# Two of four members of the middle feed-forward steps through split float32r down products, with one ring of six for the scan operands

## The reference, cut to what matters

```python
x = x + 0.5 * ffn(layernorm(x), w_gate, w_up, w_down)
x = x + attn(layernorm(x), ...)
x = x + 0.5 * ffn(layernorm(x), w_gate, w_up, w_down)

def ffn(x, w_gate, w_up, w_down):           # H = 512, I = 2048
    h = silu(x @ w_gate) * (x @ w_up)
    g = h.reshape(B, S, I // 4, 4)          # the two of largest magnitude of each four stay
    return keep_two_of_four(g).reshape(B, S, I) @ w_down

def step(h, inps):                          # the scan of the state-space part, E = 1024, N = 16
    d_l, b_l, c_l, u_l = inps
    h = exp(d_l[..., None] * A) * h + (d_l * u_l)[..., None] * b_l[:, None, :]
    return h, einsum('ben,bn->be', h, c_l)
```

## Time and profile before

| | us |
|---|---|
| median of 3 runs (3605.13 to 3610.43) | 3607.98 |
| profiled execution, time | 3602.44 |
| its span | 3600.7 |
| what lies around the span | 1.7 |
| busy: PE, DVE, POOL, ACT | 3360.2, 3027.7, 2594.9, 2061.7 |

### The profile page before, as it was taken

How to read it: one execution, slowest core, us unless ns; L and a number is a source line. 1 busy time by engine, 2 the same in 40 slices (tenths; PEclk the granted TensorE clock), 3 DMA queues, 4 the chain that set the end, 5 groups by cost and what they waited for, 6 DMA issues and landing times. The chain is left out here.

```text
span 3600.7 us, 39012 instructions
## 1 busy us (share of the span) xinstructions
PE 3360.2 (93%) x11958; PEld 2122.7 (59%) x12020; DVE 3027.7 (84%) x3597; ACT 2061.7 (57%) x2805; POOL 2594.9 (72%) x1625
## 2 busy tenths in 40 slices
PE   8999999999999999999999999988989889988899
PEld 6775566556655665566555565555545555555467
DVE  5546998788999889988898899988998988999934
ACT  5546657567565765566565675565555566454422
POOL 1316876667877779768787678868888878979913
PEclk9999999999999999999999999999999989999999
DMA  9656566657756676566665675647646556645433
GB/s 356 219 188 192 176 207 222 205 176 221 215 175 210 202 227 200 171 203 208 187 205 176 202 230 169 221 138 215 222 124 210 172 178 220 187 149 184 139 120 114
DMA packets 243470, 696.45 MB, mean 193 GB/s; under 512 B 23536, under 2 KB 23792, under 8 KB 233584
## 3 DMA queue, kind: packets, MB, share of 16 engines
q1 hardware_dynamic: 173632, 559.72, 45.1%
q10 hardware_dynamic: 69632, 134.23, 15.6%
HBM read 619.94 MB, written 76.55 MB: 193 GB/s over the span
## 5 line engine op out<-in xcount | busy, mean ns | idle before, releaser
L1381 POOL TENSOR_TENSOR scan_in<-du,scan_rows 128x512 f32<-128x512 f32 x1024 | 1312.8, 1294 | 700.9 <-DVE decay L1255 612.1
L1255 DVE TENSOR_TENSOR_SCAN decay<-decay,scan_in 128x512 f32<-128x512 f32 x1024 | 1252.4, 1223 | 157.0 <-ACT decay L865 150.9
L865 ACT ACTIVATE decay<-delta,small 128x512 f32<-128x512 f32 x1024 | 699.4, 689 | 935.4 <-DVE scan_out L1265 928.7
L1394 POOL TENSOR_TENSOR y<-y,scan_out 128x1024 f32<-128x1024 f32 x512 | 1227.0, 2397 | 0.6 <-DVE scan_out L1265 0.6
L637 PE MATMUL main<-zhi,wunit 128*128 128x512 f32 x2048 | 909.9, 444 | 62.1 <-DVE cmp L1195 38.3
L729 PE MATMUL side<-h,wdown 128*128 128x512 f32 x1760 | 801.8, 599 | 24.2 <-ACT sq L988 12.6
L639 PE MATMUL main<-zhi,wunit 128*128 128x512 f32 x2048 | 817.7, 399 | 0.0
L638 PE MATMUL main<-zlo,wunit 128*128 128x512 f32 x2048 | 816.7, 399 | 0.0
L1265 DVE TENSOR_TENSOR scan_out<-decay,scan_rows 128x512 f32<-128x512 f32 x1024 | 702.9, 686 | 27.6 <-POOL y L1394 2.2
L729 PEld LDWEIGHTS side<-h,wdown 128*128 128x128 f32 x1760 | 334.5, 191 | 392.7 <-issue 350.2
L637 PEld LDWEIGHTS main<-zhi,wunit 128*128 128x128 f32 x2048 | 390.2, 191 | 233.6 <-issue 89.5
(11 more groups left out here) (117 smaller groups left out, 3192.8 us busy)
## 6 DMA issues: line engine op xcount, KB each, us to landing
wunit<-hl_dram SPq DMA_DIRECT2D x480, 512.0 KB, 4.3
scan_rows<-bc_dram ACTq DMA_DIRECT2D x256, 512.0 KB, 5.7
wdown<-down_w_dram SPq DMA_DIRECT2D x256, 256.0 KB, 3.2
wmam<-mam_dram SPq DMA_DIRECT2D x128, 512.0 KB, 4.1
hl_dram<-wunit SPq DMA_DIRECT2D x32, 512.0 KB, 4.6
skip_dram<-skb SPq DMA_DIRECT2D x64, 256.0 KB, 4.2
delta<-skip_dram SPq DMA_DIRECT2D x16, 1024.0 KB, 6.7
wmam<-wout_dram SPq DMA_DIRECT2D x32, 512.0 KB, 4.3
```

Source lines behind the costliest of these rows:

```text
L865: nc.scalar.activation(decay[u % BANKS][:], delta[:, e, :], ACT.Exp, scale=aneg[:, e * N + n:e * N + n + 1]).then_inc(sem["decay_ready"], 1)
L1255: nc.vector.tensor_tensor_scan(decay[u % BANKS][:], decay[u % BANKS][:], db[u % INPUTS][:], 0.0, ALU.mult, ALU.add).then_inc(sem["state_re ...
L1381: nc.gpsimd.tensor_tensor(db[u % INPUTS][:], du[:, e, :], rows[m % ROWS][:, 0, :], ALU.mult).then_inc(sem["input_ready"], 1)
L1394: nc.gpsimd.tensor_tensor(y[:, e:e + 2, :], y[:, e:e + 2, :], scan_out[:, k:k + 2, :], ALU.add).then_inc(sem["sum_ready"], 1)
```

## The change

The 55 middle steps split members 0 and 1 (`SPLIT = 2`), and those halves of the down weights, into upper and lower parts. ACT copies the upper part of a member into `hmid` in the tick of its select, and that of `wdown[t]` (members 0 and 1, 128x256) into `wmid[t]` three ticks ahead of the down product; POOL subtracts one tick later, in place over `h` and `wdown` (`hlow`, `wlow`), at the head of the tick, before the tick's scan inputs. A down product becomes two float32 matmuls (members 2, 3) and six float32r ones. To make room, `scan_in` (four) and `scan_out` (six) become one ring of six: an input is written to a place, the scan reads it, `times_c` overwrites it, `sum_states` reads it. The input of unit u now also waits for the sum of unit u - 6, and LAG goes from 3 pairs to 2. The plan of ticks and units stays as it is. The diff, cut to its core (blank lines and most context left out):

```diff
@@ -31,9 +31,9 @@
 UNITS = 2 * HALF
-INPUTS, RING = 4, 6
-
-LAG = 3
+RING, AHEAD_OF_STATES = 6, 4
+
+LAG = 2
 BANKS = 2
@@ -72,6 +72,9 @@
 AHEAD_OF_SCANS = 5
+
+MIDDLE = tuple(s for s in range(4 * 2 * B) if s not in EDGE)
+SPLIT = 2
@@ -317,10 +320,10 @@
         rows = [scan_rows[:, 2 * k:2 * k + 2, :] for k in range(ROWS)]
-        scan_in = sb("scan_in", [P, INPUTS, L])
-        scan_out = sb("scan_out", [P, RING, L])
-        db = [scan_in[:, k, :] for k in range(INPUTS)]
-        pr = [scan_out[:, k, :] for k in range(RING)]
+        scan_ring = sb("scan_ring", [P, RING, L])
+        ring = [scan_ring[:, k, :] for k in range(RING)]
+        hmid = sb("hmid", [P, SPLIT, L], r32)
+        wmid = [sb(f"wmid{k}", [P, SPLIT, P], r32) for k in range(KD)]
         cv = [sb(f"cv{k}", [P, L]) for k in range(2)]
@@ -330,9 +333,12 @@
         aneg = small[:, C_AL:C_AL + KE * N]
-        hhi = nc.alloc_sbuf_tensor_at("hhi", [P, 4, L], r32, offset=base_of["scan_in"])
-        hlo = nc.alloc_sbuf_tensor_at("hlo", [P, 4, L], r32, offset=base_of["scan_out"])
-        count = nc.alloc_sbuf_tensor_at("count", [P, 3, L], bf16, offset=base_of["scan_out"] + 4 * L * 4)
+        hhi = nc.alloc_sbuf_tensor_at("hhi", [P, 4, L], r32, offset=base_of["scan_ring"])
+        hlo = nc.alloc_sbuf_tensor_at("hlo", [P, 4, L], r32, offset=base_of["scan_ring"] + 4 * L * 4)
+        count = nc.alloc_sbuf_tensor_at("count", [P, 3, L], bf16, offset=base_of["scan_ring"] + 8 * L * 4)
+
+        hlow = [nc.alloc_sbuf_tensor_at(f"hlow{k}", [P, 4, L], r32, offset=base_of[f"h{k}"]) for k in range(2)]
+        wlow = [nc.alloc_sbuf_tensor_at(f"wlow{t}", [P, 4, P], r32, offset=base_of[f"wdown{t}"]) for t in range(KD)]
         wparts = [nc.alloc_sbuf_tensor_at(f"wparts{k}", [P, 2, 4, P], r32, offset=base_of["scan_rows"] + k * 2 * L * 4) for k in range(ROWS)]
@@ -343,7 +349,7 @@
             "product_ready", "side_ready", "gate_read", "up_read", "part_ready",
-            "magnitude_ready", "compared", "counted", "selected",
+            "magnitude_ready", "compared", "counted", "selected", "mid_high_ready", "mid_split_ready", "wmid_high_ready", "wmid_split_ready",
             "member_high_ready", "member_split_ready", "down_high_ready", "down_split_ready",
@@ -396,6 +402,14 @@
                     if plan.base[s] + (3 + j // 2 if s in COUNTED else WIN_TICKS[j] + 1) == tick]
+
+        def middle_weights(tick):
+
+            return [(i, t) for i, s in enumerate(MIDDLE) for t in range(KD) if plan.base[s] + DOWN_TICKS[t] - 3 == tick]
+
+        def middle_members(tick):
+
+            return [(i, j) for i, s in enumerate(MIDDLE) for j in range(SPLIT) if plan.base[s] + WIN_TICKS[j] + 1 == tick]
@@ -725,8 +739,15 @@
                 pe.wait_ge(sem[f"down_loaded_{t}"], 16 * (s + 1))
-                for j in range(4):
-                    mm = nc.tensor.matmul(bank[:], wdown[t][:, j, :], h[s % 2][:, j, :], start=(j == 0), stop=(j == 3))
+                for j in range(SPLIT, 4):
+                    nc.tensor.matmul(bank[:], wdown[t][:, j, :], h[s % 2][:, j, :], start=(j == SPLIT), stop=False)
+                i = MIDDLE.index(s)
+                pe.wait_ge(sem["mid_split_ready"], SPLIT * (i + 1))
+                pe.wait_ge(sem["wmid_split_ready"], KD * i + t + 1)
+                for j in range(SPLIT):
+                    nc.tensor.matmul(bank[:], wmid[t][:, j, :], hmid[:, j, :], start=False, stop=False)
+                    nc.tensor.matmul(bank[:], wlow[t][:, j, :], hmid[:, j, :], start=False, stop=False)
+                    mm = nc.tensor.matmul(bank[:], wmid[t][:, j, :], hlow[s % 2][:, j, :], start=False, stop=(j == SPLIT - 1))
                 mm.then_inc(sem["side_ready"], 1)
@@ -944,10 +965,25 @@
                 if i == AHEAD_OF_SCANS:
+                    wait_job(act, ("down", MIDDLE[-1], KD - 1))
                     act.wait_ge(sem["state_ready"], B * UNITS)
                     act.wait_ge(sem["sum_ready"], B * UNITS // 2)
                 wait_selected(act, s, j)
                 nc.scalar.activation(hhi[:, j, :], h[s % 2][:, j, :], ACT.Copy).then_inc(sem["member_high_ready"], 1)
+
+            def middle_high(i, j):
+
+                s = MIDDLE[i]
+                wait_job(act, ("down", s - 1, KD - 1))
+                wait_selected(act, s, j)
+                nc.scalar.activation(hmid[:, j, :], h[s % 2][:, j, :], ACT.Copy).then_inc(sem["mid_high_ready"], 1)
+
+            def middle_down_high(i, t):
+
+                s = MIDDLE[i]
+                act.wait_ge(sem[f"down_loaded_{t}"], 16 * (s + 1))
+                wait_job(act, ("down", s - 1, t if i else KD - 1))
+                nc.scalar.activation(wmid[t][:], wdown[t][:, 0:SPLIT, :], ACT.Copy).then_inc(sem["wmid_high_ready"], 1)
@@ -1090,6 +1126,10 @@
                     down_high(i, t)
+                for i, j in middle_members(tick):
+                    middle_high(i, j)
+                for i, t in middle_weights(tick):
+                    middle_down_high(i, t)
                 upto(share(units, 1, 4).stop)
@@ -1209,6 +1249,8 @@
                     dve.wait_ge(sem["selected"], 4 * i)
+                else:
+                    wait_job(dve, ("down", MIDDLE[-1], KD - 1))
                 nc.vector.tensor_tensor(count[:, 0:2, :], cmp[:, 1:3, :], cmp[:, 3:5, :], ALU.add).then_inc(sem["counted"], 1)
@@ -1252,7 +1294,7 @@
                 dve.wait_ge(sem["input_ready"], u + 1)
-                nc.vector.tensor_tensor_scan(decay[u % BANKS][:], decay[u % BANKS][:], db[u % INPUTS][:], 0.0, ALU.mult,
+                nc.vector.tensor_tensor_scan(decay[u % BANKS][:], decay[u % BANKS][:], ring[u % RING][:], 0.0, ALU.mult,
                                              ALU.add).then_inc(sem["state_ready"], 1)
@@ -1260,9 +1302,7 @@
                 dve.wait_ge(sem["state_ready"], u + 1)
-                if u >= RING:
-                    dve.wait_ge(sem["sum_ready"], (u - RING) // 2 + 1)
-                nc.vector.tensor_tensor(pr[u % RING][:], decay[u % BANKS][:], rows[m % ROWS][:, 1, :], ALU.mult).then_inc(sem["weighted_ready"], 1)
+                nc.vector.tensor_tensor(ring[u % RING][:], decay[u % BANKS][:], rows[m % ROWS][:, 1, :], ALU.mult).then_inc(sem["weighted_ready"], 1)
@@ -1376,9 +1416,11 @@
                     pool.wait_ge(sem[f"rows_loaded_{m % ROWS}"], 16 * (m // ROWS + 1))
-                if u >= INPUTS:
-                    pool.wait_ge(sem["state_ready"], u - INPUTS + 1)
-                nc.gpsimd.tensor_tensor(db[u % INPUTS][:], du[:, e, :], rows[m % ROWS][:, 0, :], ALU.mult).then_inc(sem["input_ready"], 1)
+                if u >= RING:
+                    pool.wait_ge(sem["sum_ready"], (u - RING) // 2 + 1)
+                if u >= AHEAD_OF_STATES:
+                    pool.wait_ge(sem["state_ready"], u - AHEAD_OF_STATES + 1)
+                nc.gpsimd.tensor_tensor(ring[u % RING][:], du[:, e, :], rows[m % ROWS][:, 0, :], ALU.mult).then_inc(sem["input_ready"], 1)
@@ -1391,12 +1433,23 @@
                     pool.wait_ge(sem["sum_ready"], p - HE // 2 + 1)
-                nc.gpsimd.tensor_tensor(y[:, e:e + 2, :], y[:, e:e + 2, :], scan_out[:, k:k + 2, :], ALU.add).then_inc(sem["sum_ready"], 1)
+                nc.gpsimd.tensor_tensor(y[:, e:e + 2, :], y[:, e:e + 2, :], scan_ring[:, k:k + 2, :], ALU.add).then_inc(sem["sum_ready"], 1)
             def member_low(i, j):
                 pool.wait_ge(sem["member_high_ready"], 4 * i + j + 1)
                 nc.gpsimd.tensor_tensor(hlo[:, j, :], h[EDGE[i] % 2][:, j, :], hhi[:, j, :], ALU.subtract).then_inc(sem["member_split_ready"], 1)
+
+            def middle_low(i, j):
+
+                s = MIDDLE[i]
+                pool.wait_ge(sem["mid_high_ready"], SPLIT * i + j + 1)
+                nc.gpsimd.tensor_tensor(hlow[s % 2][:, j, :], h[s % 2][:, j, :], hmid[:, j, :], ALU.subtract).then_inc(sem["mid_split_ready"], 1)
+
+            def middle_down_low(i, t):
+
+                pool.wait_ge(sem["wmid_high_ready"], KD * i + t + 1)
+                nc.gpsimd.tensor_tensor(wlow[t][:, 0:SPLIT, :], wdown[t][:, 0:SPLIT, :], wmid[t][:], ALU.subtract).then_inc(sem["wmid_split_ready"], 1)
@@ -1430,6 +1483,10 @@
                     down_low(i, t)
+                for i, j in middle_members(tick - 1):
+                    middle_low(i, j)
+                for i, t in middle_weights(tick - 1):
+                    middle_down_low(i, t)
                 for u in plan.units_at[tick]:
                     scan_input(u)
                     if u % 2 == 1:
```

## The result

The changed kernel takes 3901.6 us (median of 4 runs, 3897.6 to 3903.7) against 3606.6 for the kernel before: ratio 1.0822, 95% interval 1.0809 to 1.0836, 295 us slower. The prediction of 3636 (3562 to 3706) had the sign and missed the size: 34 us over the profiled execution were forecast, 295 measured. The profiled execution's span is 3895.8 us.

A forecast was written before the change was run, and what follows sets the result against it. PE was taken to set the pace for the first two thirds, DVE after. From 3602.4 us, -50 (PE) +37 (overfull windows) +20 (stalls) +10 (ACT) +4 (port) +13 (lost lead) gave +34: 3636 us, range 3562 to 3706.

The forecast's parts named there:

- PE's saving: Down products of middle steps: 0.32 us less each, 69 us over 55 steps, booked at -50 for 40 steps with room.
- The ring: Scan buffers: sums waiting for times_c and LAG 2 taken to cost 0, bounds 0 and 20 us.
- POOL's work: New subtractions in middle steps: 5.5 us a step, 303 us over 55 steps (280 to 425).
- The wait behind the selects: POOL at base+5 waits for DVE's selects: 3.5 us stall, 73 us in 30 steps, booked at 20.
- overfull windows: 15 of 53 middle-step windows where POOL's old plus new work exceeds the window, by 37 us together.
- the waits for the weight copies: Lead lost at base+4, base+6 and base+7, where weight halves head POOL's tick: 0.25 us a step, +13.
- ACT: New copies, 2.9 us a step, 160 us in all, lengthen DVE's waits for decays: +10, bounds 0 and 45.
- The shared port: Busier POOL delays DVE operations on two SBUF tiles: +4 us, bounds 0 and 15.
- The clock: Last third: PE's pauses might pull down its granted clock, making the full loss worse; no size given.
- the rival of a full loss: Stalls paid in full at base+5, PE's saving given back: +73 and +37, 3712 us, chance 0.17.
- The one of a gain: Stalls vanish into DVE's waits for PE, PE's saving stays: about 3570 us, chance 0.28.
- The one of a dearer float32r: float32r inside a float32 accumulation has its own price on PE: +84 us, 3686, part of the 0.17.

The follow-up runs named there:

- run 4: Changed kernel with neither weights nor members split after the first middle step; PE's new matmuls and the ring stay; 3602.1 us, ratio 0.9989.
- the ring alone: Kernel before with only the ring of six and LAG 2; middle-step down products stay float32; 3610.1 us, ratio 1.0012.
- run 8: As run 4, no splits, but all four members in float32r, read from the first step's upper parts; 3596.1 us, ratio 0.9976.
- run 13: Changed kernel with members split only in the first middle step, weight copies two ticks earlier, weight subtractions behind the tick's scan inputs; 3647.8 us.
- run 2: Changed kernel with down weights split only once, before the first middle step; members split as in the changed kernel; 3787.1 us.
- run 3: Changed kernel with members split only once, in the first middle step; weights split as in the changed kernel; 3812.0 us.
- run 7: Changed kernel with weight copies two ticks earlier, weight subtractions behind the tick's scan inputs, and member subtractions moved to DVE; 3747.6 us.
- run 5: Changed kernel with ACT's copies of the weight halves two ticks earlier, all work and POOL's subtraction ticks kept; 3869.7 us.

## Why the prediction was wrong, step by step

The terms of the sum against the runs: PE's saving, booked at -50 us, is worth -8 (run 4 against the ring alone). The ring, booked at 0, costs 5. All that the splits bring to ACT and POOL was booked at 84 us (37, 20, 10, 4 and 13) and costs 299 (the changed kernel against run 4). So most of the miss, 215 us, lies in the price of the splits, and 42 in PE's saving.

**PE's saving** was right as work and wrong as time. A down product takes 3.12 us (443.19 to 446.31, which is the last start and one pitch of 0.23) against 3.44, the 0.32 forecast:

```profile
443.19 1.88 PE L743 MATMUL side<-h,wdown 128*128 128x512 f32 x4
444.51 0.80 PE L748 MATMUL side<-hmid,wmid 128*128 128x512 f32 x1
...
446.08 0.39 PE L750 MATMUL side<-hlow,wmid 128*128 128x512 f32 x1
```

The sum booked -50 us for 40 steps; against the ring alone run 4 gives -8, and run 8 some -13 for twice as much. The step that failed first is this one: from "PE is busy for 96%" I concluded that PE sets the pace. PE, DVE and ACT are levelled, and each waits now and then for another: relief of PE alone is worth 3 to 8 us, of DVE alone 41 of 89, of ACT's table loads 37, and PE's is worth 20 only on top of ACT's. In a plain step (step 7) DVE is busy for 39.1 of 40.8 us, and 1.2 of the rest is waiting for decays; PE's 39.0 stood beside it, not ahead of it.

**POOL's work** was right: 0.79 us for a weight half (0.74 forecast), 1.32 for a member, 317 us in all (303).

```profile
L1452 POOL TENSOR_TENSOR wlow<-wdown,wmid 128x256 fp32r<-128x256 f32 x220 | 174.1, 793 | 344.4 <-ACT wmid L986 325.1 <-DVE decay L1297 19.2
L1447 POOL TENSOR_TENSOR hlow<-h,hmid 128x512 fp32r<-128x512 f32 x110 | 142.9, 1320 | 122.3 <-ACT hmid L979 122.3
```

With next to no wait, the weight halves' 174 us of it cost 46 us together with ACT's copies (run 13).

**The wait behind the selects** was named, placed and sized rightly for a plain step (3.5 us forecast, 3.59 seen), and then booked at a quarter of its worth. This is the step that cost most. I counted 73 us, halved what fell outside the overfull windows, and took 20. The changed kernel shows 229.7 us at scans, and 28.1 more where DVE's gating of y (line 1335) waits for POOL's last sum, 1.9 before. Put to their ticks by the plan, 81.3 of the 229.7 us stand at `base+5`, so the 73 were about right and the discount was wrong. Another 17.7 stand at `base+4` and 91.2 at `base+6` and `base+7`, where the prediction had 13. With members alone (run 2) it is 58.9 at `base+5`; with weights alone (run 3) 11.3 there and 74.1 at the two ticks behind. Three things were missing. First, the waits for the weight copies, at the heads of three more ticks of each step: the prediction said of them only 0.25 us a step. Runs 3 and 13 price them, with what they do to DVE's busy time, at 164 us when they stand alone. Second, a lead of four units is lost at each gate and has to be won back, out of the little that POOL is faster than DVE in the dense ticks as far as the rows tell; step 8 shows further stalls of 0.71, 0.68, 1.64 and 0.70 us behind the first. Third, POOL's standing still and its work are in series. The 15 "overfull windows" took the larger of two times where the sum of POOL's work and its idle time at the gate was due, as step 7 shows (43.0 and 7.2 us in 50.2).

**ACT** was put at 10 us. Its copies took 0.40 and 0.63 us as forecast, but DVE's waits for decays went down, from 151 to 135. Its part is that of the one that POOL waits for (447 us). What its copies cost as work was not tried alone.

**The ring** was right at 0: 5 us, within 0 to 20.

**The shared port** was mis-sized. I took 4 us with an upper bound of 15; DVE's busy time grew by 108 us. Two groups hold most of it (busy us, mean ns of one), the first two rows from the kernel before, the other two from the changed one:

```profile
L1295 DVE TENSOR_TENSOR y<-y,delta 128x512 f32<-128x512 f32 x64 | 51.9, 871 | 13.2 <-DMA delta<-skip_dram 11.3 <-POOL y L1394 1.9
L1159 DVE TENSOR_TENSOR zlo<-zm,zhi 128x512 fp32r<-128x512 f32 x64 | 49.5, 834 | 0.0
L1335 DVE TENSOR_TENSOR y<-y,delta 128x512 f32<-128x512 f32 x64 | 96.2, 1561 | 29.2 <-POOL y L1436 28.1 <-DMA delta<-skip_dram 1.1
L1199 DVE TENSOR_TENSOR zlo<-zm,zhi 128x512 fp32r<-128x512 f32 x64 | 81.3, 1329 | 0.4 <-ACT zhi L945 0.4
```

They are DVE instructions with two SBUF operands, and nothing in them was changed. The error was to scale with POOL's busy share. What counts is whether POOL is at work just then. Of these 128 instructions, those with no POOL instruction beside them take 0.68 us in both kernels, those with one 1.96 before and 1.86 after; there were 17 of the second kind before and there are 83 now. A POOL that is behind works straight on through the ticks where it used to stand waiting for DVE. This agrees with the rule of the Trainium skill that the prediction weighed ("SBUF — State Buffer", Who interferes with whom); how often the two meet in a kernel, only the rows tell. The scans, whose decay lies in PSUM, are untouched as forecast: 1.223 us in the mean before, 1.225 after. What part of the 295 us the port makes was not tried apart from the rest, and this rival of the waits stays open in size. In run 7 the same effect on 110 new instructions is 0.67 us each (1.355 less the 0.68 of such an operation undisturbed), 74 us.

**The clock** is the last term. PE's busy time grew although its work fell: the mean granted clock of the execution is 0.946 against 0.979. From 452.44 on, after 5.97 us of waiting for DVE, the matmuls follow each other at 0.43 us, from 459.81 on again at 0.23:

```profile
452.44 0.79 PE L651 MATMUL main<-zhi,wunit 128*128 128x512 f32 x1 [5.97 <-DVE cmp L1235]
453.03 0.63 PE L652 MATMUL main<-zlo,wunit 128*128 128x512 f32 x1
453.45 0.63 PE L653 MATMUL main<-zhi,wunit 128*128 128x512 f32 x1
...
460.05 0.40 PE L653 MATMUL main<-zhi,wunit 128*128 128x512 f32 x1
460.28 0.39 PE L651 MATMUL main<-zhi,wunit 128*128 128x512 f32 x1
```

Two windows around these rows, columns as above, have the granted clock at 0.50 and 1.00, which are the two levels of 1.2 and 2.4 GHz:

```profile
452.40:456.00 3.60, 3.56 (x8) 2.81 (x9) 3.60 (x5) 1.36 (x3) 3.47 (x3) 0.50 0.02 5
459.40:462.00 2.60, 2.53 (x11) 2.07 (x12) 2.50 (x4) 2.48 (x4) 1.72 (x2) 1.00 0.90 297
```

Here the low clock follows a stall. What it adds to the 295 us no run parts; the rival of a full loss named it without a number.

**The rivals.** The one of a gain fell: DVE did wait, and PE had nothing to gain by. The one of stalls paid in full decided as it said, no gain on PE and stalls that stay. Its price of 110 us (3712) was 190 short of the 3901.6; the waits for the weight copies, the port and the clock are what it left out, and their shares are not parted. The one of a dearer float32r fell with run 8 and the 3.12 us. What could have been read beforehand: each subtraction at the head of a POOL tick has a partner on ACT in the tick before, and POOL's tick is tied to ACT's at all four of them. A lead of four units is 1.7 ticks where 2.3 units stand in a tick (1024 units on 448 ticks). I followed it through only one of the four gates.

## What to carry to other kernels

An engine that runs ahead of the others in its own queue does so only until its first instruction that needs something of the present: before work is given to its idle time, list every new wait with the tick of its producer, and count the lead as lost at each. With the copy early and the subtraction behind the work that others wait for, the same instructions cost 46 us instead of 210 (runs 13 and 3). And a busy share of 96% doesn't show which engine sets the pace; leaving out the helpers' work (run 4) shows in one run that the saving, with the ring, is worth 3 us.

## What the runs showed of the hardware

A wait taken away from a queue can reappear at the next gate in nearly its full length: 325 us at the weight copies became 241 us more at the members (run 5), with 32 us of gain. DVE's subtraction of two SBUF tiles of 128x512 took 0.68 us with no POOL instruction beside it and 1.55 in the mean with one (run 7), while scans with one operand in PSUM kept their 1.22 us. Going from float32 to float32r inside an accumulation shows no gap (0.32 us saved as worked out).
